# Attention over edge tiles: scores through memory in their own layout, row moments as running sums of ScalarE

## The reference

```python
x = _layernorm(x + _L0_gnn_ref(...)); x = _layernorm(x + _L1_gnn_ref(...))
x = _layernorm(x + _L2_gnn_ref(...)); x = _layernorm(x + _L3_gnn_ref(x, batch0, edge_index, L3_gnn_W))
# in _L1_gnn_ref, after the batch norm (scale and shift of each column):
out = jnp.where(out >= 0, out, SLOPE * out); out = out + x
# in _L3_gnn_ref:
q, k, v = jnp.split(x @ W, [Fqk, 2 * Fqk], axis=-1)
aw = jnp.einsum('ehf,ehf->eh', qs, ks)            # scores, 8 for each edge
m = jax.ops.segment_max(aw, src, num_segments=n)
e = jnp.exp(aw - m[src]); denom = jax.ops.segment_sum(e, src, num_segments=n)
out = jax.ops.segment_sum((e / denom[src])[:, :, None] * vs, src, num_segments=n)
```

## Time and profile before

| | us |
|---|---|
| median of 3 runs | 2539.53 |
| profiled execution | 2559.03 |
| its span | 2557.3 |
| TensorE busy | 1912.6 (75%) |
| VectorE busy | 1569.5 (61%) |
| ScalarE busy | 1055.6 (41%) |
| GpSimd busy | 932.2 (36%) |
| weights of the stage asked for, to its last store issued | 1730 to 2460 |

### The profile page before, as it was taken

The page is one execution under the profiler, slowest core; times in us unless marked ns, Lnnn a source line. Parts: engine busy times, 40 slices in busy tenths (PEclk is TensorE's granted clock), DMA queues, the critical chain, the costliest instruction groups (busy, mean ns, idle before and its releaser), DMA issues. The chain is left out here.

```text
span 2557.3 us, 23979 instructions
## 1 busy us (share of the span) xinstructions
PE 1912.6 (75%) x5496; PEld 953.9 (37%) x5496; DVE 1569.5 (61%) x2664; ACT 1055.6 (41%) x2019; POOL 932.2 (36%) x1055
## 2 busy tenths in 40 slices
PE   5999995999999999999978603545766666677400
PEld 3444442444444444444434302332333333333200
DVE  5465451777777777777742437976555555555564
ACT  2344342555555555555543212434443333343122
POOL 2211012666665666666646244642011111100023
PEclk9999997999999999999998855556878788888755
DMA  7731024444444444444426342426444444433433
GB/s 250 260 105 38 13 33 117 153 155 145 155 160 149 146 161 157 146 152 161 152 103 199 46 106 69 87 56 245 94 134 114 110 116 116 116 116 108 114 131 111
DMA packets 170013, 326.07 MB, mean 128 GB/s; under 512 B 39889, under 2 KB 53106, under 8 KB 169686
## 3 DMA queue, kind: packets, MB, share of 16 engines
q1 hardware_dynamic: 138438, 244.22, 28.1%
q0 software_dynamic: 28160, 76.53, 13.9%
q10 hardware_dynamic: 3344, 4.51, 0.5%
HBM read 185.35 MB, written 139.84 MB: 127 GB/s over the span
## 5 line engine op out<-in xcount | busy, mean ns | idle before, releaser
L661 PE MATMUL d_p_h<-w3a,d_xT 128*128 128x512 f32 x640 | 290.6, 597 | 25.4 <-DMA d_xT<-in_xT 25.4
L661 PE MATMUL d_p_o<-d_w,d_uT 128*128 128x512 f32 x640 | 289.7, 595 | 3.0 <-ACT d_uT L736 3.0
L661 PE MATMUL d_p_p<-d_wr,d_x1T 128*128 128x512 f32 x640 | 290.6, 597 | 0.0
L818 DVE TENSOR_TENSOR d_zz<-d_yg,d_xbeta 128x512 f32<-128x512 f32 x80 | 138.6, 1732 | 98.8 <-POOL d_yg L869 98.8
L550 POOL TENSOR_SCALAR d_small<-d_mv 128x1 f32<-128x1 f32 x160 | 81.8, 511 | 304.9 <-DVE d_mv L787 155.0
L661 PEld LDWEIGHTS d_p_h<-w3a,d_xT 128*128 128x128 f32 x640 | 122.6, 192 | 180.7 <-issue 180.7
L661 PEld LDWEIGHTS d_p_o<-d_w,d_uT 128*128 128x128 f32 x640 | 121.9, 191 | 156.6 <-issue 152.1
L1489 POOL DMA_INDIRECT f_sums<-sum,index x40 | 40.1, 1003 | 365.5 <-PE f_p_T L1525 354.5
L1594 PE MATMUL f_p_S<-f_both,same_src 128*128 128x260 f32 x80 | 36.8, 607 | 170.4 <-DVE f_both L1796 170.4
L661 PEld LDWEIGHTS d_p_p<-d_wr,d_x1T 128*128 128x128 f32 x640 | 116.6, 192 | 117.1 <-issue 117.1
L729 ACT ACTIVATE d_yn<-d_y,d_small 128x512 f32<-128x512 f32 x80 | 65.1, 813 | 230.4 <-POOL d_small L555 230.4
(11 more groups left out here) (250 smaller groups left out, 4265.1 us busy)
## 6 DMA issues: line engine op xcount, KB each, us to landing
state<-d_empty SPq DMA_DIRECT2D x80, 264.0 KB, 2.1
sum<-m_tile_sum SPq DMA_DIRECT2D x10, 2048.0 KB, 7.7
d_xT<-in_xT SPq DMA_DIRECT2D x80, 256.0 KB, 2.7
d_z<-sum SPq DMA_DIRECT2D x80, 256.0 KB, 2.9
d_x<-in_x SPq DMA_DIRECT2D x80, 256.0 KB, 3.0
x<-d_x SPq DMA_DIRECT2D x80, 256.0 KB, 2.0
p<-d_p SPq DMA_DIRECT2D x80, 256.0 KB, 2.0
pair_p<-p SPq DMA_DIRECT2D x40, 512.0 KB, 7.0
```

The lines of the kernel that those rows point to most:

```text
L661: last = nc.tensor.matmul(out[:, :], lhsT[:, c, :], w[:, c, :], start=(c == 0), stop=(c == KB - 1))
L818: nc.vector.tensor_tensor(zz[b][:, :], yg[b][:, :], xbeta[b][:, :], ALU.add).then_inc(zz_done, 1)
```

## The change

1. The scores are written as they lie, 8 numbers (32 bytes) of each partition in one run, so that memory holds them edge by edge. The read back is the same size, and VectorE's addition in `tile_maximum` reads `spread` with a stride of 8 numbers, to have heads outside again.
2. `pair_moments` on VectorE keeps only the residual (now `pair_residual`). Statistics, aggregation and negation go. `pair_normalise` on ScalarE makes the sum of each row as the running sum of a Copy, the negative mean, and the sum of squared deviations as the running sum of a Square with the negative mean as bias; `reciprocal_deviation` divides by 512 in its scale. Two scratch tiles take the elementwise results.
3. On VectorE the first pair's `pair_leaky` moves ahead of the tile maximum, and its residual ahead of the weighing.
4. AHEAD goes from 6 to 5 buffers of gathered sums.

```diff
-def pair_moments(nc, k, dve, j):
+def pair_residual(nc, k, dve, j):
...
                                    in1=k.pair_p[b][:, :, :], op0=ALU.mult, op1=ALU.add).then_inc(k.pair_y, 1)
-    dve.wait_ge(k.pair_y, j + 1)
+
+
+def pair_normalise(nc, k, act, j):
+
+    b = j % 2
+    rows, total, neg, ss = k.pair_rows[b], k.pair_total[b], k.pair_neg[b], k.pair_ss[b]
+    act.wait_ge(k.pair_y, j + 1)
     for s in range(2):
-        nc.vector.bn_stats(k.pair_stats[b][:, s, :], k.pair_rows[b][:, s, :]).then_inc(k.pair_st, 1)
+        if j:
+            act.wait_ge(k.pair_squares, 2 * j - 1 + s)
+        nc.scalar.activation(k.pair_scratch[s][:, :], rows[:, s, :], ACT.Copy, accum_out=total[:, s:s + 1]
+                             ).then_inc(k.pair_totals, 1)
+    act.wait_ge(k.pair_totals, 2 * j + 2)
+    nc.scalar.activation(neg[:, :], total[:, :], ACT.Copy, scale=-1.0 / D).then_inc(k.pair_mean, 1)
+    act.wait_ge(k.pair_mean, j + 1)
     for s in range(2):
-        dve.wait_ge(k.pair_st, 2 * j + s + 1)
-        nc.vector.bn_aggr(k.pair_mv[b][:, s, :], k.pair_stats[b][:, s, :]).then_inc(k.pair_moments, 1)
-    dve.wait_ge(k.pair_moments, 2 * j + 2)
-    nc.vector.tensor_scalar(k.pair_neg[b][:, :], k.pair_mv[b][:, :, 0], -1.0, None, ALU.mult).then_inc(k.pair_ready, 1)
...
+        nc.scalar.activation(k.pair_scratch[s][:, :], rows[:, s, :], ACT.Square, bias=neg[:, s:s + 1],
+                             accum_out=ss[:, s:s + 1]).then_inc(k.pair_squares, 1)
+    act.wait_ge(k.pair_squares, 2 * j + 2)
+    reciprocal_deviation(nc, k, act, ss[:, :], neg, k.pair_rstd[b][:, :], k.pair_shift[b], k.pair_sc, 4 * j, norms=3,
+                         over=D)
...
-        T, AHEAD, STEPS = EDGE_TILES, 6, EDGE_TILES + 4
+        T, AHEAD, STEPS = EDGE_TILES, 5, EDGE_TILES + 4
...
-                    sp.dma_start(k.aw_rows[t, :].rearrange("(h p) -> p h", h=HEADS), k.scores[:, t, :]
+                    sp.dma_start(k.aw_rows[t, :].rearrange("(p h) -> p h", h=HEADS), k.scores[:, t, :]
                                  ).then_inc(aw_out, 16)
...
-                nc.vector.tensor_tensor(cand[:, :, :], spread[:, :, :],
+                nc.vector.tensor_tensor(cand[:, :, :], spread.rearrange("p (e h) -> p h e", h=HEADS),
                                         away[:, :].rearrange("p (a e) -> p a e", a=1).to_broadcast([P, HEADS, P]),
                                         ALU.add).then_inc(cand_done, 1)
...
+                if HERE[step]:
+                    pair_leaky(nc, k, dve, pair)
                 if 0 <= d < T:
                     tile_maximum(d)
                 if HERE[step]:
-                    pair_leaky(nc, k, dve, pair)
+                    pair_residual(nc, k, dve, pair)
                 if 0 <= d < T:
                     weigh_values(d)
-                if HERE[step]:
-                    pair_moments(nc, k, dve, pair)
                 if a < T:
                     softplus(a)
                 for j in range(pair + 1, pair + HERE[step]):
                     pair_leaky(nc, k, dve, j)
-                    pair_moments(nc, k, dve, j)
+                    pair_residual(nc, k, dve, j)
```

More of the change, by code:

```diff
@@ L1078, in tail_buffers @@
     k.pair_p, k.pair_x1, k.pair_rows = (two(n, [P, 2, D]) for n in ("p", "x1", "rows"))
-    k.pair_stats, k.pair_mv = two("stats", [P, 2, 6]), two("mv", [P, 2, 2])
-    k.pair_neg, k.pair_rstd, k.pair_shift = (two(n, [P, 2]) for n in ("neg", "rstd", "shift"))
+    k.pair_total, k.pair_neg, k.pair_ss, k.pair_rstd, k.pair_shift = (
+        two(n, [P, 2]) for n in ("total", "neg", "ss", "rstd", "shift"))
+    k.pair_scratch = two("scratch", [P, D])
     k.eps = sb("eps", [P, 2])
@@ L1084, in tail_buffers @@
         [sem(f"{n}{i}") for i in range(2)] for n in ("p_in", "x1_in", "gone"))
-    k.pair_scaled, k.pair_shifted, k.pair_leaky, k.pair_y, k.pair_st, k.pair_moments, k.pair_ready, k.pair_sc, k.pair_out = (
-        sem(n) for n in ("scaled", "shifted", "leaky", "y", "st", "moments", "ready", "sc", "out"))
+    k.pair_scaled, k.pair_shifted, k.pair_leaky, k.pair_y, k.pair_totals, k.pair_mean, k.pair_squares, k.pair_sc, k.pair_out = (
+        sem(n) for n in ("scaled", "shifted", "leaky", "y", "totals", "mean", "squares", "sc", "out"))
 def norm_factors(norms):
@@ L1096, in set_eps, with reciprocal_deviation @@
     nc.gpsimd.memset(k.eps[:, 1:2], norm_factors(3)[1]).then_inc(k.eps_set, 1)
-def reciprocal_deviation(nc, k, act, var, neg_mean, rstd, shift, done, base, norms=1):
+def reciprocal_deviation(nc, k, act, var, neg_mean, rstd, shift, done, base, norms=1, over=1):
     n = var.shape[-1]
     col = 0 if norms == 1 else 1
-    nc.scalar.activation(rstd, var, ACT.Ln, bias=k.eps[:, col:col + 1], scale=norm_factors(norms)[0]).then_inc(done, 1)
+    nc.scalar.activation(rstd, var, ACT.Ln, bias=k.eps[:, col:col + 1], scale=norm_factors(norms)[0] / over
+                         ).then_inc(done, 1)
     act.wait_ge(done, base + 1)
@@ L1153, in pair_moments @@
                                    in1=k.pair_p[b][:, :, :], op0=ALU.mult, op1=ALU.add).then_inc(k.pair_y, 1)
-    dve.wait_ge(k.pair_y, j + 1)
-    for s in range(2):
-        nc.vector.bn_stats(k.pair_stats[b][:, s, :], k.pair_rows[b][:, s, :]).then_inc(k.pair_st, 1)
-    for s in range(2):
-        dve.wait_ge(k.pair_st, 2 * j + s + 1)
-        nc.vector.bn_aggr(k.pair_mv[b][:, s, :], k.pair_stats[b][:, s, :]).then_inc(k.pair_moments, 1)
-    dve.wait_ge(k.pair_moments, 2 * j + 2)
-    nc.vector.tensor_scalar(k.pair_neg[b][:, :], k.pair_mv[b][:, :, 0], -1.0, None, ALU.mult).then_inc(k.pair_ready, 1)
 def pair_normalise(nc, k, act, j):
     b = j % 2
-    act.wait_ge(k.pair_ready, j + 1)
-    reciprocal_deviation(nc, k, act, k.pair_mv[b][:, :, 1], k.pair_neg[b], k.pair_rstd[b][:, :], k.pair_shift[b],
-                         k.pair_sc, 4 * j, norms=3)
+    rows, total, neg, ss = k.pair_rows[b], k.pair_total[b], k.pair_neg[b], k.pair_ss[b]
+    act.wait_ge(k.pair_y, j + 1)
     for s in range(2):
-        row = k.pair_rows[b][:, s, :]
+        if j:
[5 more added lines that the diff above has]
+    act.wait_ge(k.pair_mean, j + 1)
+    for s in range(2):
+        nc.scalar.activation(k.pair_scratch[s][:, :], rows[:, s, :], ACT.Square, bias=neg[:, s:s + 1],
[3 more added lines that the diff above has]
+                         over=D)
+    for s in range(2):
+        row = rows[:, s, :]
         nc.scalar.activation(row, row, ACT.Identity, bias=k.pair_shift[b][:, s:s + 1],
@@ L1399, in values_phase @@
         slots = lambda first, n: k.same_dst[:, first:first + n, :].rearrange("p t e -> p (t e)")
-        spread, prod, q = slots(0, 8).rearrange("p (h e) -> p h e", h=HEADS), slots(8, KB), slots(12, KB)
+        spread, prod, q = slots(0, 8), slots(8, KB), slots(12, KB)
         srcT = k.same_dst[:, 16:20, :]
@@ L1467, in _ @@
                         sp.wait_ge(cand_done, t)
-                    sp.dma_start(spread[:, :, :].rearrange("p h e -> p (h e)"),
+                    sp.dma_start(spread,
                                  k.aw_rows[t:t + 1, :].to_broadcast([P, P * HEADS])).then_inc(spread_in, 16)
```

## The result

The changed kernel takes 2417.53 us, the median of 4 runs (2413.64 to 2420.71), against 2537.9 us of the kernel before, timed beside it (4 runs, 2536.0 to 2550.1): a ratio of 0.9515, 95% interval 0.9482 to 0.9549. The forecast was 2426. Its profiled execution took 2420.71 us (span 2419.0), 138.3 less than that of before. Of these, 135.7 lie in the attention stage, which went from 733.1 to 597.4 us (from the first gather of sums to the first gather of the last stage).

The account below looks back on a forecast made before the run. Bound: attention's loop through the scores' write and read back. A and B together, 64.45 to 51.9 us, save 12.5 nine times (112); with 4 at step 4 and 3 lost opening, 113 in all: 2446 profiled, 2426 median, range 2390 to 2475.

Parts of the forecast that it names:

- A: Attention-stage step with one pair of plain rows on VectorE, alternating with B; forecast to fall from 35.85 to 28.0 us.
- B: Attention-stage step with two pairs on VectorE, alternating with A; forecast to fall from 28.6 to 23.85 us.
- The write: SyncE's 4 KB write of scores to memory: from 11.21 to 3.1 us, bounds 1.9 and 5.3.
- The early leaky part in A: VectorE holds A's maximum for the pair's load, 0.37 + 6.3 us, then 3.77 more: 10.4 us behind the spread, not 5.5.
- From maximum to F: Start of the tile maximum on VectorE to F: 8.1 us, where A had 11.6 and B 10.5.
- F: The end of the softplus, the point from which the prediction counts each attention step.
- The stride: The maximum's addition on VectorE reading at a stride of 32 B: taken as zero extra cost.
- The rival's doubling: Rival: the stride doubles the maximum's addition on VectorE, 1.22 us more in 20 steps, 2450 us; chance 0.12.
- ScalarE's pair: Normalising one pair on ScalarE goes from 2.5 to 6.1 us, its added moments 3.6 (3.0 to 4.2).
- SyncE's queue: B's write queues behind A's second pair's store: issued at F + 5.6, then 4.6 us with 1.5 for running behind it.
- Opening and tail: Ends of the attention stage: opening taken as 3 us lost (bounds 0 and 10), tail as 0 (-5 to +4).
- The rival with the write as slow as before: Rival: write time doesn't hang on the number of runs; A 36.1, B 30.5, so 2560 us; chance 0.05.

Follow-up runs that it names:

- layout_only: The kernel before with part 1 alone (scores written as they lie, strided addition): 2373.73 us, ratio 0.9325.
- leaky_behind: The changed kernel with the first pair's leaky part back behind the tile maximum (part 3 undone): 2382.4 us, ratio 0.9365.
- layout_ahead5: layout_only with part 4, 5 buffers of gathered sums instead of 6: 2376.44 us, ratio 0.9347.
- before_again: The kernel before, unchanged, profiled a second time: 2544.18 us in one run, attention stage 719.4 us.
- old_write: The changed kernel with part 1 undone, the write again 1024 runs of 4 bytes and the addition contiguous: 2590.22 us, ratio 1.0183.
- loads_first: The changed kernel, but SyncE issues the loads of pairs ahead of the write of the scores: 2391.35 us, ratio 0.9403.
- reduce_strided: The changed kernel, but the addition keeps memory's order and the maximum reads with the stride: 2415.37 us in one run.
- layout_moved: layout_only, with the second pair of each B step made on VectorE behind the next step's scores and new maximum: 2349.83 us, ratio 0.9245.
- behind_defer: leaky_behind, with the store of an A step's second pair issued behind the next step's spread: 2384.55 us, ratio 0.9375.

## Why the prediction was right, point by point

- **The bound** was read rightly: the write's time is nearly the whole gain. From before to layout_only the write loses 9.7 us in A and 9.8 in B, where the two steps lose 18.2.
- **The write**: 1.55 us in A for 3.1, and 2.43 in B behind the store for 4.6. The first lies below my lower bound of 1.9 (the landing of 128 KB was no floor for 4 KB), the second within its bounds. The time fell nearly as the number of runs, 1024 to 128 for 11.17 to 1.55. But two layouts don't tell number, length and place in memory of the runs apart, so which of them sets the time stays open. The estimate from the Trainium skill ("DMA: Bandwidth & Descriptors", section "Anatomy of one DMA — SWDGE (gpsimd) path"), 2.0 us, was nearer than my 3.1, and the trace lies below it too; that section is on transfers issued by GpSimd, and this one is SyncE's.
- **The early leaky part in A**: the new wait was as forecast, the spread to the maximum 9.41 for 10.4; in the step shown the leaky part starts 5.2 us after the issue of its load, for 6.3. In B "it vanishes in the wait for the spread" was wrong: f_y came late from ScalarE, so VectorE began it 2.0 us behind the spread's issue and ended it 5.6 behind, while in leaky_behind the spread lands after 4.4; 6.45 for 5.55 in the mean.
- **From maximum to F**: 8.81 and 9.91 for 8.1. 0.78 of it is the stride. In B the rest is TensorE's path: VectorE waits for the values (0.72 us in the step shown) and ScalarE for the first product, which the normalisation ahead of the query copy holds (46.0 us of TensorE's waits in 19 steps, 2.4 a step, for 2.5).
- **The stride** taken as zero was wrong: 2.00 us for 1.22, above the 1.3 us that the prediction named as a sign of being wrong, at most some 16 us in 20 steps. The rival's doubling was too much. The row L1296 with 96 elements didn't stand for 1024. The Trainium skill ("SBUF — State Buffer", section "Door 1: The DMA port swizzle") was right in direction; it gives no price.
- **ScalarE's pair**: 5.65 us (1969.63 to 1975.28) for 6.1. The Copy takes 0.62, the Square with a bias 0.72, the tiny Copy 0.20, a read of the accumulator 0.19.
- **SyncE's queue**: B's write at F + 5.27 for 5.6, behind a store issue that ends at 1993.26.
- **Part 4** taken as zero holds: layout_ahead5 can't be told from layout_only.
- **The sum**: A 26.03 for 28.0, B 24.07 for 23.85, 50.1 for 51.9 in both. The write came out smaller by 3.7 us in both, the load by 1.0, and the way from maximum to F larger by 2.5, the wait for the maximum in B by 0.9; the ways from F to the write were 0.5 shorter. The errors partly cancel.
- **Opening and tail**: the first write is 77.5 us into the stage for 74.0, so 3.5 lost for 3. From the last write to the end 39.5 us for 48.9: 9.4 gained where I took 0. I had left the write of the last tile out of the sum.
- **The total**: 135.7 us in the stage are 129.8 between first and last write, 9.4 behind it and 3.5 lost ahead. By its own profiled execution the kernel came 25 us below the 2446 of the sum; by medians 8.5 below 2426. The difference is that the profiled execution of before lay 19.5 us above its median and that of after 3.2; 13.7 of it are slower transfers in that one execution (before_again). That only 8.5 us remain is in part luck. Both steps together took 50.1 us, 1.8 less than in the sum; but in the execution that I read, both steps of before were 64.3 us, 1.6 more than in before_again (62.7). So 62.7 less 50.1 is 12.6, next to the 12.5 of the sum, though neither end of it was right.
- **The rival with the write as slow as before** would have been near: old_write has A 35.8 and B 31.4 for 36.1 and 30.5. Its 2560 is 30 low, in part since the double step of before is nearer to 62.7 than to 64.3.

What the prediction didn't ask is whether each part earns its place: the sum had a gain of 12.5 us per double step for four parts, and never one for part 1 alone. Its own terms had the answer for part 3: with the leaky part behind the maximum, A's spread to maximum is 5.55 for 10.4, and VectorE has 2.6 + 3.77 + 1.26 + 0.7 + 0.85 = 9.2 us to F for 8.1, so A would be 24.3 for 28.0 (measured: 22.95 for 26.03).

## What to carry to other kernels

Price each part of a change against the change without it, not only against the kernel before: here one part brings 167 us, and the others give 44 back. Moving work from a busy engine to an idle one brought nothing here, since the places it landed in are on the chain; ScalarE had 61 of 100 us free, yet a normalisation stood ahead of the query copy, or of the logarithms, in both places tried. And when a long wait is taken away, fill what is left of it with work that nobody waits for, behind the operation that feeds the loop: the second pair moved behind the scores was worth 24 us.

## What the runs showed of the hardware

- A write of 4 KB from 128 partitions takes, issue to issue and in the mean, 10.5 to 11.3 us as 1024 runs of 4 bytes and 1.4 to 1.55 us as 128 runs of 32. Behind a 512 KB store just issued it takes 12.0 in the old layout (old_write) and 2.4 in the new one, and with loads of 512 KB issued just ahead 3.8 to 5.0 in the new layout (loads_first).
- float32 read at a stride of 32 bytes over 1024 elements costs VectorE 0.78 us more than contiguous (2.00 for 1.22), in the addition (after) and in the maximum (reduce_strided) alike.
- ScalarE's running sum costs one read of the accumulator of 0.19 us, part of which overlaps the next operation; VectorE's took 0.083.
- TensorE's granted clock rose from 0.81 of full in the stage before to 0.95 in the changed kernel and 0.98 in layout_moved (1950 to 2050 us). It still falls in places. Two first products behind an idle time of 2.42 us take 2.07 us, at 0.50 (the lower of its two levels) from 1988.0 to 1990.2, as before; they take 1.02 where TensorE came straight from other products (1972.80 in behind_defer). A wait of 2.14 us ahead of the values did not slow them: 3.70 us at 1975.91, at a clock of 1.00.
